# Experts' weights as outer products of two small exponentials, rows normalized on ScalarE, maxima split by two-input operations, and the order of work written anew

## What is computed

```python
xn = layernorm(x)
out = x + attention(xn) + mlp(xn) + experts(xn)
# attention: 16 heads of 8, rotary embedding, causal softmax, projection
# mlp: silu(xn @ Wg + bg) * (xn @ Wu + bu) @ Wd + bd, 512 wide
# experts, for each token and each of 4 heads:
sx = xn @ Wq_x @ keys_x        # 64 values; only the first 8 name an expert below 512 on their own
sy = xn @ Wq_y @ keys_y        # 64 values
top 8 of sx, top 8 of sy -> best 8 of the 64 sums sx_i + sy_j
w = silu(xn . down_embed[64 i + j]) * softmax(best 8)
experts = sum of w * up_embed[64 i + j]      # indices of 512 and above count as the last one
```

## Time and profile before

| | |
|---|---|
| median of 3 runs | 778.15 us (777.24 to 779.65) |
| profiled execution | 773.43 us, span 771.6 us |
| PE busy | 665.6 us (86%) |
| DVE busy | 643.7 us (83%) |
| ACT busy | 537.9 us (70%) |
| POOL busy | 493.2 us (64%) |
| mean granted PE clock | 0.964 |
| HBM traffic | 27.2 MB, 35 GB/s |

### The profile page before, as it was taken

The page is one execution under the profiler, slowest core; times in us unless marked ns, Lnnn a source line. Parts: engine busy times, 40 slices in busy tenths (PEclk is TensorE's granted clock), DMA queues, the critical chain, the costliest instruction groups (busy, mean ns, idle before and its releaser), DMA issues.

```text
span 771.6 us, 16962 instructions
## 1 busy us (share of the span) xinstructions
PE 665.6 (86%) x5788; PEld 290.2 (38%) x5788; DVE 643.7 (83%) x1369; ACT 537.9 (70%) x811; POOL 493.2 (64%) x588
## 2 busy tenths in 40 slices
PE   3847678799999998999789999999889998898896
PEld 2523234334333344434334344433334344333232
DVE  3129899988898989998898989998998989998751
ACT  3523445578985885779777795779877785879883
POOL 6422776867665867777566776776666766476660
PEclk9776969999999999999999999999999999999998
DMA  8322400210021000121111000031110000100100
GB/s 157 90 89 66 85 3 21 69 58 2 21 91 51 17 2 22 28 100 66 39 42 30 2 3 21 6 117 66 43 43 17 2 2 2 30 2 1 30 1 14
DMA packets 29115, 29.93 MB, mean 39 GB/s; under 512 B 5730, under 2 KB 27202, under 8 KB 27458
## 3 DMA queue, kind: packets, MB, share of 16 engines
q1 hardware_dynamic: 25832, 27.66, 12.1%
q10 hardware_dynamic: 3200, 1.18, 0.8%
HBM read 18.81 MB, written 8.39 MB: 35 GB/s over the span
## 4 chain that ended last, share of the span: by engine, by line
DVE 36%; PE 34%; issue 15%; POOL 7%; ACT 4%; DMA 2%; POOLq 0%; DVEq 0%; SPq 0%; ACTq 0%
DVE pmax L871 18%; PE ybank L999 6%; DVE ssum L793 6%; PE ring L1084 5%; PE ring L976 4%; PE ring L951 4%; PE ring L1066 3%; PE ring L1005 3%; PE ring L1074 2%; POOL ssum L609 2%; PE ring L1059 2%; POOL coef L636 2%; PE ring L1038 2%; DMA xin<-in_L_attn_x 2%; DVE negmax_pad L850 1%
## 5 line engine op out<-in xcount | busy, mean ns | idle before, releaser
L759 ACT ACTIVATE pT<-ring 128x1024 f32<-128x1024 f32 (+3 forms) x384 | 298.4, 808 | 125.6 <-PE ring L983 74.9
L871 DVE TENSOR_REDUCE pmax<-ring 128x2 f32<-128x1024 f32 (+3 forms) x304 | 343.0, 1159 | 39.8 <-PE ring L961 24.6
L636 POOL TENSOR_TENSOR coef<-coef,ssum 128x512 f32<-128x512 f32 x128 | 171.1, 1353 | 140.2 <-DVE ssum L793 140.2
L999 PE MATMUL ybank<-pT,vaug 128*32 128x512 f32 (+3 forms) x1536 | 156.4, 501 | 0.3 <-ACT yT L747 0.2
L976 PE MATMUL ring<-qs,ks 59*128 59x512 bf16 (+3 forms) x768 | 121.8, 330 | 29.7 <-DVE pmax L871 19.9
L951 PE MATMUL ring<-ks,qs 56*128 56x512 bf16 (+3 forms) x768 | 115.0, 337 | 37.4 <-DVE pmax L871 22.5
L609 POOL TENSOR_TENSOR ssum<-sim 128x512 f32<-128x512 f32 x128 | 129.9, 1046 | 0.1
L976 PEld LDWEIGHTS ring<-qs,ks 59*128 59x128 bf16 x768 | 39.6, 93 | 169.2 <-DVE pmax L871 59.8
L793 DVE TENSOR_SCALAR ssum<-ssum,best,zinv 128x512 f32<-128x512 f32 x128 | 98.6, 802 | 1.9 <-ACT coef L720 1.3
L720 ACT ACTIVATE coef<-ssum,nbest 128x512 f32<-128x512 f32 x128 | 88.3, 715 | 10.7 <-DVE coef L805 5.4
L951 PEld LDWEIGHTS ring<-ks,qs 56*128 56x128 bf16 x768 | 36.7, 95 | 109.3 <-DVE pmax L871 37.9
(11 more groups left out here) (118 smaller groups left out, 866.6 us busy)
## 6 DMA issues: line engine op xcount, KB each, us to landing
parts_scratch<-parts SPq DMA_DIRECT2D x16, 384.0 KB, 3.6
qs<-parts_scratch SPq DMA_DIRECT2D x16, 192.0 KB
ks<-parts_scratch SPq DMA_DIRECT2D x16, 192.0 KB
xin<-in_L_attn_x SPq DMA_DIRECT2D x8, 256.0 KB, 8.7
qs<-parts_scratch SPq DMA_DIRECT2D x16, 128.0 KB
ks<-parts_scratch SPq DMA_DIRECT2D x16, 128.0 KB
rows<-in_L_attn_x SPq DMA_DIRECT2D x8, 256.0 KB, 3.4
out<-rows SPq DMA_DIRECT2D x8, 256.0 KB, 2.7
```

Of the source, the lines that this page charges most:

```text
L636: g.tensor_tensor(coef4[:, h, :], coef4[:, h, :], ssum[:, h, :], ALU.mult).then_inc(weighed, 1)
L759: a_.activation(pT[:, n % NPT, 2 * pr:2 * pr + 2, q0:CHUNK], pair_of(t)[:, :, q0:CHUNK], ACT.Exp, scale=SCALE).then_inc(ring_copied_scalar, 1)
L871: v.tensor_reduce(pmax[:, it, k0 // CHUNK, 2 * pairs[0]:2 * pairs[-1] + 2] .rearrange("p (j e) -> p e j", e=2), pair_of(t)[:, :, 0:w * len ...
L999: ins = t_.matmul(ybank[32 * j:32 * j + 32, q0:CHUNK], vaug[:, b % 2, kt, v0:v0 + 32], pT[:, n % NPT, j, q0:CHUNK], start=kt == 0, stop=kt ...
```

## The change

Five things change.

- "spread" and "weigh" go. Since exp(sx_i + sy_j - m) is a product, "offsets" (POOL, 2 instructions a tile) subtracts each head's largest sx and sy, "exps" (ACT, one instruction of 4 x 72 elements) takes the exponentials, and "outer" (POOL) multiplies the 8 exponentials of sx by zinv and then makes the 512 products of a head, 4 instructions, into coef4. nbest goes.
- "keep" is one scalar_tensor_tensor for a head: (ssum >= eighth best) times coef4, into coef4, with two SBUF inputs. It waits for pairs and for its head's product. "pairs" and "coef" wait for keep in place of weigh.
- "xn" moves to ACT (Identity with a scale and a bias); POOL computes minus mean times rstd in "ln" by two more instructions.
- The maxima are split without a multiplication by -1 and without a copy or cast: a maximum of two inputs writes each bf16 part, and negmaxT is copied with a scale of -1.
- SEQUENCE is another list of 1984 tasks in place of 2048. Its head and its end stand below.

```diff
-    "spread": each(B, NT, RH), "keep": each(B, NT, RH), "mlp": each(B, NC, 2 * NF),
+    "keep": each(B, NT, RH), "mlp": each(B, NC, 2 * NF),
-                                       "weigh", "coef", "total", "experts")})
+                                       "offsets", "exps", "outer", "coef", "total", "experts")})
...
-ln xn load expand xT expand weave*2 ropeT load ropeT weave*2 turned expand rot swapped setup rest third swapped
-setup first rot setup second turned setup*17 keep_parts expand ln ropeT xT first load_parts rest gate xn second
-gate keep_parts swapped*2 third ropeT down*2 turned v turned rot load_parts up keep_parts first rot second
-rest*2 first gate down gate third second up v up max*11 negate down up negmaxT third keep_parts load_parts
-negmax load_parts sim top max best max cand zinv dif load scores weights pairs max scores weigh spread*2 max
-keep*2 rows spread keep spread keep scores*2 values cand pairs max*2 sim scores*2 top scores load values max
...
-scores values scores dif scores values weights y scores*2 experts spread pairs spread zinv keep values scores*2
-values scores experts spread scores keep scores values keep values scores*2 spread scores values*2 keep scores*2
-mlp*2 ycopy weigh mlp scores*2 total scores values y experts values scores coef scores mlp*3 scores*2 values*2
-scores*2 mlp*2 scores values scores*3 values*3 ycopy rows y yT proj outT store
+load keep_parts load ln xn expand weave*2 expand weave*2 keep_parts expand ln ropeT xT ropeT swapped rot turned
+setup*5 swapped setup turned first expand setup*2 rest rot load_parts setup*2 third setup second setup top first
+rest setup*3 third setup*3 second xn setup*2 load_parts xT sim ropeT pairs turned swapped turned ropeT swapped
+best offsets zinv cand rot dif exps keep_parts rot outer weights sim first v gate down top cand down first down
+load_parts gate v keep second weights keep rest*2 keep_parts keep*2 best max*8 zinv max*3 total up negate third
+dif exps keep second gate offsets down up coef keep*3 negmaxT experts up gate up scores total third scores pairs
...
+scores*2 keep outer up scores offsets values best cand total store scores*3 values exps y experts weights coef
+scores*3 zinv values*2 pairs scores dif scores mlp keep*2 scores negmax scores values scores*3 values*3 scores*2
+keep*2 outer coef mlp experts ycopy mlp scores*3 total values*2 scores*2 mlp experts y scores rows scores*2
+values*2 scores*3 values scores*2 values*3 ycopy mlp store mlp y mlp yT mlp proj outT store
...
+        nmean = sb("nmean", [P, NT])
-        nbest = sb("nbest", [P, RH])
+        expxy = sb("expxy", [P, RH, XI + NKEYS])
+        expx = sb("expx", [P, RH, XI])
...
-        pool.wait_ge(var_ready, n + 1)
-        g.tensor_tensor(rstd[:, tiles], vareps[:, tiles], half_neg[:, :], ALU.pow).then_inc(rstd_ready, 1)
+        pool.wait_ge(var_ready, 3 * n + 1)
+        g.tensor_tensor(rstd[:, tiles], vareps[:, tiles], half_neg[:, :], ALU.pow).then_inc(var_ready, 1)
+        pool.wait_ge(var_ready, 3 * n + 2)
+        g.tensor_tensor(nmean[:, tiles], meanvar[:, tiles, 0], rstd[:, tiles], ALU.mult).then_inc(var_ready, 1)
+        pool.wait_ge(var_ready, 3 * n + 3)
+        g.tensor_tensor(nmean[:, tiles], nmean[:, tiles], minus[:, :], ALU.mult).then_inc(rstd_ready, 1)
     elif kind == "rot":
...
     elif kind == "pairs":
...
-        pool.wait_ge(weighed, RH * i)
+        pool.wait_ge(kept_ready, RH * i)
         for h in range(RH):
...
-        pool.wait_ge(spread_ready, RH * i)
...
-        g.tensor_tensor(nbest[:, :], best[:, :, 0], minus[:, :], ALU.mult).then_inc(dif_ready, 1)
-    elif kind == "weigh":
+    elif kind == "offsets":
...
+        copied(pool, ("sim", b, t[2]))
+        pool.wait_ge(top_ready, i + 1)
+        pool.wait_ge(outer_ready, RH * i)
+        g.tensor_tensor(expxy[:, :, 0:XI], sim[:, 0:RH, 0:XI], wide(xs[:, :, 0:1], XI), ALU.subtract)\
+            .then_inc(offsets_ready, 1)
+        g.tensor_tensor(expxy[:, :, XI:], sim[:, RH:2 * RH, :], wide(ys[:, :, 0:1], NKEYS), ALU.subtract)\
+            .then_inc(offsets_ready, 1)
+    elif kind == "outer":
+        i = b * NT + t[2]
+        pool.wait_ge(expxy_ready, i + 1)
+        pool.wait_ge(zinv_ready, i + 1)
+        g.tensor_tensor(expx[:, :, :], expxy[:, :, 0:XI], zinv[:, :].unsqueeze(2).to_broadcast([P, RH, XI]),
+                        ALU.mult).then_inc(expx_ready, 1)
+        pool.wait_ge(expx_ready, i + 1)
+        pool.wait_ge(coef_ready, i)
         for h in range(RH):
-            pool.wait_ge(kept_ready, RH * i + h + 1)
-            g.tensor_tensor(coef4[:, h, :], coef4[:, h, :], ssum[:, h, :], ALU.mult).then_inc(weighed, 1)
+            g.tensor_tensor(coef4[:, h, :].rearrange("p (i j) -> p i j", i=XI),
+                            expx[:, h, :].unsqueeze(2).to_broadcast([P, XI, NKEYS]),
+                            expxy[:, h:h + 1, XI:].to_broadcast([P, XI, NKEYS]), ALU.mult)\
+                .then_inc(outer_ready, 1)
     elif kind == "coef":
...
-        pool.wait_ge(weighed, RH * (i + 1))
+        pool.wait_ge(kept_ready, RH * (i + 1))
...
+    elif kind == "xn":
+        c = t[2]
+        act.wait_ge(rstd_ready, b * NC + c + 1)
+        for n in range(c * TPC, (c + 1) * TPC):
+            a_.activation(xin[:, n, :], xin[:, n, :], ACT.Identity, scale=rstd[:, n:n + 1],
+                          bias=nmean[:, n:n + 1]).then_inc(xn_ready, 1)
     elif kind == "first":
...
     elif kind == "negmaxT":
...
-        a_.activation(negmaxT[:, :], ringb[BANK[t][0]][0:3 * H // 2, 0:CHUNK], ACT.Copy)\
+        a_.activation(negmaxT[:, :], ringb[BANK[t][0]][0:3 * H // 2, 0:CHUNK], ACT.Copy, scale=-1.0)\
...
     elif kind == "sim":
...
+        act.wait_ge(offsets_ready, 2 * i)
...
     elif kind == "weights":
...
-        act.wait_ge(dif_ready, 2 * i + 1)
+        act.wait_ge(dif_ready, i + 1)
...
-    elif kind == "spread":
-        i, h = b * NT + t[2], t[3]
-        act.wait_ge(dif_ready, 2 * (i + 1))
-        act.wait_ge(pairs_ready, RH * i + h + 1)
-        act.wait_ge(coef_ready, i)
-        a_.activation(coef4[:, h, :], ssum[:, h, :], ACT.Exp, bias=nbest[:, h:h + 1])\
-            .then_inc(spread_ready, 1)
+    elif kind == "exps":
+        i = b * NT + t[2]
+        act.wait_ge(offsets_ready, 2 * (i + 1))
+        a_.activation(expxy[:, :, :], expxy[:, :, :], ACT.Exp).then_inc(expxy_ready, 1)
     elif kind == "down":
...
     if kind == "top":
...
+        dve.wait_ge(offsets_ready, 2 * i)
         for a in range(2 * RH):
...
     elif kind == "best":
...
-        dve.wait_ge(dif_ready, 2 * i)
+        dve.wait_ge(dif_ready, i)
...
         for h in range(RH):
...
-        dve.wait_ge(kept_ready, RH * i)
+        dve.wait_ge(expx_ready, i)
...
     elif kind == "keep":
...
-        dve.wait_ge(zinv_ready, i + 1)
-        dve.wait_ge(spread_ready, RH * i + h + 1)
-        v.tensor_scalar(ssum[:, h, :], ssum[:, h, :], best[:, h, KPH - 1:KPH], zinv[:, h:h + 1],
-                        ALU.is_ge, ALU.mult).then_inc(kept_ready, 1)
+        if h == 0:
+            dve.wait_ge(pairs_ready, RH * (i + 1))
+        dve.wait_ge(outer_ready, RH * i + h + 1)
+        v.scalar_tensor_tensor(out=coef4[:, h, :], in0=ssum[:, h, :], scalar=best[:, h, KPH - 1:KPH],
+                               in1=coef4[:, h, :], op0=ALU.is_ge, op1=ALU.mult).then_inc(kept_ready, 1)
     elif kind == "total":
...
         for n in range(c * TPC, (c + 1) * TPC):
...
-    elif kind == "xn":
-        dve.wait_ge(stats_done, TPC * (b * NC + c + 1))
-        dve.wait_ge(rstd_ready, b * NC + c + 1)
-        for n in range(c * TPC, (c + 1) * TPC):
-            v.tensor_scalar(xin[:, n, :], xin[:, n, :], meanvar[:, n, 0:1], rstd[:, n:n + 1],
-                            ALU.subtract, ALU.mult).then_inc(xn_ready, 1)
     elif kind in ("turned", "swapped"):
...
-def negated(b, st):
+def split_maxima(b, st):
...
-    m = pmax[:, n, 0, hs]
-    if c > 0:
-        k = steps.mark(v.tensor_tensor(mrest[:, :, :], m, pmax[:, n, 1, hs], ALU.max))
-        steps.need(k)
-        m = mrest[:, :, :]
-    k = steps.mark(v.tensor_scalar(rmax[:, :, :], m, -1.0, None, ALU.mult))
-    steps.need(k)
+    m0, m1, whole, rest = [ap.rearrange("p n (j e) -> p n e j", e=2) for ap in
+                           (pmax[:, n, 0, hs], pmax[:, n, c, hs], rmax[:, :, :], mrest[:, :, :])]
...
-    pj = [ap.rearrange("p n (j e) -> p n e j", e=2) for ap in (rmax[:, :, :], mrest[:, :, :])]
-    k = steps.mark(v.tensor_copy(negmax[:, :, :, 0, :], pj[0]))
+    if c > 0:
+        steps.mark(v.tensor_tensor(whole, m0, m1, ALU.max))
+    else:
+        whole = m0
+    k = steps.mark(v.tensor_tensor(max_parts[:, :, :, 0, :], m0, m1, ALU.max))
...
-    k = steps.mark(v.tensor_tensor(pj[1], pj[0], negmax[:, :, :, 0, :], ALU.subtract))
+    k = steps.mark(v.tensor_tensor(rest, whole, max_parts[:, :, :, 0, :], ALU.subtract))
...
-    k = steps.mark(v.tensor_copy(negmax[:, :, :, 1, :], pj[1]))
```

(32 more changed lines are left out.)

166 lines of the change are left out of this document (73 added, 93 removed).

## The result

The changed kernel takes 810.12 us (median of 4 runs, 807.29 to 812.61), the kernel before 777.69 on the same chip (776.25 to 779.65): ratio 1.0421, 95% interval 1.0385 to 1.0457. It is slower by 32 us, where 768 us were forecast, and it lies outside the range of 748 to 790. The profiled execution has a span of 809.9 us, 38.3 more than before.

What follows compares the result with a forecast made beforehand. TensorE and VectorE, both 91% busy, share the bound in the long middle, between a head waiting for first maxima and a tail. Terms +12 +4 -6 -3 -4 -3 -8 -2 = -10 us on 778.15 gave 768; range 748 to 790.

Steps and rivals of the forecast that it cites:

- the weight: Work added to VectorE costs about its share of the chain: 47% for the keep's line, 43% for VectorE as a whole.
- (1): VectorE becomes the bound: keeps wait 0.45 us each beside outer products, mean 1.19 us, time 787; chance 0.29.
- forecast of the keep: VectorE's keep: own time 0.74 us, wait 0.33 us, mean near 1.07; +12 and +4 us on the end.
- The maxima: VectorE's maxima: one instruction fewer in 16 groups, -3 us of busy time, waits as before; -4 us on the end.
- the forecast of 661: VectorE's busy time in us: 643.7 + 25.6 + 9 - 3 - 9 - 5, 87% of the new span.
- The head: Start of the kernel: k load issued at 31.0 instead of 39.3, first maxima at about 45.7; -8 us.
- Rival 3: Head's gain isn't kept: first maxima at 46, but VectorE or second-batch loads set the pace; 776, chance 0.13.
- the 3 us of gain: ScalarE: net -58 us of work, busy near 480 us; worth -3 us on the end.
- Its gain of 6 us on the end: GpSimd: keeps its 64% busy, but weigh leaves the chain for expx and the first product; -6 us.
- Normalization: Moved off VectorE, which loses 9.1 us; -3 us taken on the end.
- Two-input maxima as a form: The maxima step's effect on the end: -4 us, ends -8 and +4.
- The tail: End of the kernel: last four experts' matmuls go into TensorE's waits behind the last attention group; -2 us.

Runs made afterwards that it cites:

- experiment 12: Kernel before with the normalization moved to ScalarE and the two-input split of the maxima together: 771.58 us, ratio 0.9913.
- experiment 3: Kernel before with the normalization alone moved to ScalarE, one normalization standing earlier in the list: 775.54 us, ratio 0.9970.
- experiment 9: Changed kernel with the 128 outer products cut from 512 to 8 elements each, other weights zero: 764.57 us, ratio 0.9849 to the kernel before.
- experiment 4: Kernel before with the two-input split of the maxima alone: 775.59 us, ratio 0.9961.
- experiment 8: Changed kernel with the one-input keep of before, the experts' weights left unmasked: 785.40 us, ratio 1.0111 to the kernel before.
- experiment 2: Kernel before with one more VectorE maxima instruction behind every second keep, 64 in all: 786.12 us, ratio 1.0095.
- experiment 1: Kernel before with one more VectorE instruction behind each keep, 128 in all: 813.09 us, ratio 1.0453.
- experiment 11: Changed kernel with the first stage's loads of q and k cut to half their bytes: 805.12 us, ratio 1.0358 to the kernel before.
- experiment 5: Changed kernel with the maxima split as before (multiplication by -1, casts): 821.29 us, ratio 1.0559 to the kernel before.
- 6: All operations of the changed kernel in the list of the kernel before: 856.48 us, ratio 1.1007 to the kernel before.
- 7: All operations of the kernel before in the list of the changed kernel: 952.17 us, ratio 1.2255 to the kernel before.
- 10: Changed kernel in which a tile's first keep waits for all four of its outer products: 848.76 us, ratio 1.0904 to the kernel before.
- both crossings: New operations in the old list, 856.48 us, and old operations in the new list, 952.17 us.

## Why the prediction was wrong

Span less VectorE's busy time, in the profiled executions:

| kernel | VectorE busy | span | difference |
|---|---|---|---|
| old with both parts (12) | 630.6 | 771.0 | 140.4 |
| old, normalization on ScalarE (3) | 633.8 | 772.1 | 138.3 |
| new, short products (9) | 636.3 | 764.1 | 127.8 |
| old, new maxima (4) | 640.9 | 772.5 | 131.6 |
| before | 643.7 | 771.6 | 127.9 |
| new, one-input keep (8) | 650.4 | 782.3 | 131.9 |
| old, half padding (2) | 652.3 | 787.6 | 135.3 |
| old, full padding (1) | 673.9 | 806.8 | 132.9 |
| new | 681.5 | 809.9 | 128.4 |
| new, half of the first loads (11) | 683.4 | 803.5 | 120.1 |
| new, old maxima (5) | 686.1 | 820.1 | 134.0 |

From 636 to 686 us the end follows VectorE within 8 us, with the operations and list of either kernel, but for 11, whose head is shorter. The other exceptions are 6, 7 and 10, not in the table, which wait openly, and the two kernels of the old list below 640 us, where the end stays near 771.

**The step that failed: the weight.** "Work added to VectorE costs about its share of the chain" took 47% and 43% as the price. In busy time against medians, what is added costs 0.86 (8.6 us, experiment 2), 1.2 (30.2 us, experiment 1) and, in the change itself, 32.4 / 37.8 = 0.86; taken out of the changed kernel it gives back 24.7 / 31.1 = 0.79 (experiment 8) and 1.0 (experiment 9). What is taken from the kernel before gives different amounts: 1.0 for 2.8 us (experiment 4), 0.3 for the 9.9 us that went to ScalarE (experiment 3), 0.5 for the 13.1 of both (experiment 12). So the direction alone doesn't set the price. The low 0.3 may come from TensorE, which is as busy as VectorE, or from ScalarE's new work; that is not shown. Of the rivals, (1), VectorE becomes the bound, is what happened, at 810 beyond its 787. Its condition, a mean keep of 1.1 us, wasn't met: the keep has 0.987. So the forecast of the keep was too high (own time 0.746 for 0.74, wait 0.24 for 0.33), and the price of a microsecond was half of what it is.

**The term that was mis-sized: the waits of the small operations.** The maxima were put at -3 us of VectorE, with waits as before; they came to +14. The sum over heads had no term; it is +4.9. VectorE's busy time was forecast at 661 and is 681.5, 20.5 more: these two gave 22, the keep took back 11, and of the other 10, 5 are the last term of the forecast of 661, a -5 that none of its steps gives; the remaining 5 lie in small groups and in how much of the records overlap, which I didn't follow. The rows on L842 in the earlier trace rows had shown the mechanism; I counted which keeps would meet a product and not what else stood in the 4.2 us. A dependent series is the worst case: each operation loses the rest of the product that runs, and the next one meets the next product (timeline above). By the Trainium skill, "SBUF — State Buffer", section "Who interferes with whom", just such two-input instructions contend with a GpSimd instruction that reads SBUF; the trace agrees, with 0.97 us for 0.19.

**The head.** The issue of the k load came at 31.59, as worked out (31.0). TensorE's first scores came at 53.23 (53.96 before) and not at 45.7, and the first maxima at 54.30 (55.03 before), since the step took the issue for what sets the landing. The q load is issued at 27.58, before at 24.3, and the k load streams behind it; experiment 11 shows that it is bytes. The head gave about 1 us instead of 8. By experiment 11, scores that start 10 us earlier are worth 5 at the end. Rival 3 doesn't describe this: it had the first maxima at 46.

**What held, and what came to nothing.** ScalarE: 489.1 us for some 480; the 3 us of gain are not to be seen. GpSimd: 507.7 for 488, half of it since the products have a mean of 1.15 and not 1.04: VectorE holds them up too. Its gain of 6 us on the end didn't come; its share of the chain rose from 7 to 11%. Normalization: -9.1 of busy time, and -2.8 on the end for -3 (experiment 3). Two-input maxima as a form: -3 for -4. The tail is 38 us for 37, without the 2 us of gain.

With the measured numbers the sum is: VectorE +37.8 at full price, head -1, so +37 in the profiled executions, where +38.3 was found. From the forecast's -10 this is 47 us away, in three parts. With the forecast busy time (+17) the full price adds 8, since the sum had +9 for it (12 + 4 - 4 - 3); the 20.5 us of missed busy time add 20; and 18 are the gains of GpSimd, ScalarE, head and tail (19), of which 1 came. Why those of GpSimd, ScalarE and tail came to nothing no run shows; where VectorE sets the end, as the table has it, work taken from the others gives nothing. The medians differ by 32 only, since the profiled execution of before (773.4) was 4.3 us under the median of 777.69 and that of the changed kernel (811.8) 1.7 us above its own. That the sum comes out within 2 us is partly luck, since it rests on one execution of each.

What stays open: no run separated the order of the new list from its operations, since both crossings came out far slower than either kernel. The 11 us for 4.6 us of busy time in experiment 5 has no account. That TensorE's lower clock follows from its waits for VectorE, and is no cause of its own, rests on the order of events in the trace (last section) and on no run. And why more keeps are caught under the full padding (58) than under the half (50) or before (49) was not looked into by a run of its own.

## What to carry to other kernels

The share of the chain is no price. Here, with two engines both at 91% and coupled by a ring of banks, work added to one counted nearly in full, and work removed counted anything from a third to the whole: price the two directions apart, and ask whether the engine's idle time can shrink at all (here it stayed at 128 us). Before long operations are set back to back on GpSimd, list every small two-input operation that VectorE has in that stretch, and count one long operation for each of a dependent series.
